# Routing one pass sooner, with halved choices and shorter steps for the last four batches

## The chip, the cores and the metric

One core of a Trainium2 chip runs the whole program. Its engines, each with a queue of its own that it works through in order, are TensorE (PE in the rows; its weight loads are PEld), VectorE (DVE), ScalarE (ACT), GpSimd (POOL) and SyncE (SP, which here only starts transfers). They wait for one another by semaphores that are written out by hand. The metric is device time in microseconds (us). All times inside the program are counted from the start of the profiled span.

## The reference, cut to what matters

`x` is 32 batches of 128 tokens by 128 features, `ctx` the same. Four blocks are added to `x` one after the other:

```python
x = x + attention_16_heads(layernorm(x), ctx)        # first attention
x = x + experts(layernorm(x))                        # 8 experts, one chosen for each token
x = x + attention_16_heads_of_64(layernorm(x), ctx)  # second attention
x = x + gated_block(layernorm(x))                    # quantised weights
```

The experts' choice (the routing) works on `i = layernorm(x)` after the first attention:

```python
num = einsum('bsd,ed->bse', i, waff)
aff = num / (norm(i) * norm(waff) + 1e-9)
tcr = one_hot(argmax(softmax(aff)))                  # the token's expert
```

Each token then goes through its expert's two matrices, if its affinity ranks high enough in its batch.

## The kernel before, in words

The program has three stages. The first is the first attention together with the routing, the second sorts the tokens by expert and runs 39 tiles of 128 tokens through the experts, the third is the second attention with the gated block.

**The first stage** is `attention_routing_block`. It runs 32 passes, one for each batch b, and every engine has its own loop over b with its own order of work. In a pass PE forms the scores of batch b, their maxima for batch b + 1 and the sums over values of batch b, and also what is left of batch b - 1: four transpositions back (`back_transposes`, L439), one more (`o_transpose`, L444) and the output product (`output`, L450). VectorE takes maxima (L720), normalises (L726, L729), adds the residual (`residual`, L735) and takes its mean and variance (`residual_stats`, L739 and L741). ScalarE copies (L533, L557, L562) and takes exponentials (L552).

**The routing of a batch r** follows its attention by some passes. It is a row of small steps on four engines:

- POOL: `route_norm(r)` adds a constant to the variance (L238), takes the power -1/2 (L240), and scales the batch to `xy` (the program's `xn2`, L244). From batch SCALED = 27 on VectorE scales (`route_scale`, L746).
- PE: `route_transpose(r)` (L336), in pass r + 4. ScalarE copies it (`route_copy`, L533). PE: `affinity(r)`, the product with `waff` (L367). VectorE copies that (`num_copy`, L628).
- For a group of batches (0 to 7, 8 to 15, 16 to 23, 24 to 27, 28 to 31): POOL computes `denominators` (L253 to L263, two powers and products), VectorE the choice in ten or so small steps (`choose`: reciprocal L634, affinity L642, and so on to the choice itself, `tcrb`, L663, and the running counts `seen`, L673), PE the place of each token (`places`, L385 to L390), VectorE the position (`locate`, L699 to L710).
- POOL: `scatter(r)` (L270) sends the batch's 128 rows to `sorted_x` in HBM, to the positions found. It sends one batch in a pass at first, two from pass 24, three from pass 29.

The tables `close_at` and `group_at` say in which pass a group's places and choice come. The choice of group 2 stands whole in VectorE's pass 27, between the residual and the copy of q (`q_spread`, L622); `route_transpose` in PE's next pass waits for that copy, since both use one PSUM bank. The choices of the last two groups come after the loops.

**The last batches.** After its loop PE works on the rest of batch 31 and on the routing of batches 29 to 31, and in between it adds up a part of the experts' constants (`expert_sums_part`, L1003, four matmuls for an expert). The count of tokens per expert (`countp`, L384) comes ahead of the places of group 4. POOL computes `denominators(4)`, and then scatters the last seven batches.

**Behind it** SP starts 18 loads for the third stage as soon as the statistics of batch 31 are known, then waits for all scatters and for the list of tiles and loads the first tiles of `sorted_x` (`e_xt`). PE has three products of weights (L1657, L1660, L1665) and then the tiles.

Of the kernel before, what the change touches and what calls it, by code (L numbers as in the profile page):

```python
# [13 lines left out]
P = 128  # L14
# [30 lines left out]
def routing_state(nc, space, ctx):  # L45
# [7 lines left out]
    def sem(name):  # L53
# [10 lines left out]
        seen=sb("seen", [P, 6, E], BF16),  # L64
        place=sb("place", [P, G, E]), posf=sb("posf", [P, B]), pos_s=sb("pos_s", [P, B], I32),
        zeros=sb("zeros", [P, 704]))
    s = {n: sem(n) for n in ("w_in", "set", "wsq", "wsum_done", "wsum", "wn", "rs2", "den", "xn2", "xnt", "xnT",
                             "num_done", "num", "choice", "place_done", "place", "z_out", "scat")}
# [3 lines left out]
def attention_routing_block(nc, ctx, space, consts, x, ctxT, w, wr, x_res, xn2, stats2, psum, dram):  # L72
# [19 lines left out]
    LATE = 28  # L92
# [49 lines left out]
    countp = xp[:, S + 16:S + 16 + E]  # L142
# [51 lines left out]
    def pool_part(g, after_setup, before_loop):  # L194
# [51 lines left out]

        def denominators(q):
# [39 lines left out]
        for b in range(B):  # L287
# [4 lines left out]
            if b >= 2:  # L292
                route_norm(b - 2)
# [19 lines left out]
    def tensor_part(pe, expert_sums_part):  # L313
# [4 lines left out]
        def x_transpose(b, s):  # L318
# [5 lines left out]
            wait(pe, rsem["num"], b - 5)  # L324
            nc.tensor.transpose(first_x(b), xn[:, s, :], ident[:]).then_inc(xt_done, 1)

        def route_transpose(r):
            pe.wait_ge(rsem["xn2"], r + 1)
            if r >= LATE:
                pe.wait_ge(mx_ready, 4 * B)  # L330
                pe.wait_ge(rsem["xnT"], r)
            else:
                pe.wait_ge(qz_ready, min(r + 6, B))
            if r == B - 5:
# [25 lines left out]
        def affinity(r):  # L360
# [4 lines left out]
            elif r + 4 in close_at:  # L365
                pe.wait_ge(rsem["place"], 4 * close_at[r + 4] + 1)
            nc.tensor.matmul(nump[r >= LATE], rt["xnT"][:, r % 2, :], rt["waffT"][:], start=True, stop=True).then_inc(rsem["num_done"], 1)  # L367

        def places(q):
# [5 lines left out]
            if q < SPREAD:  # L375
                pe.wait_ge(rsem["xnT"], z + 4)
            elif z + 5 <= B:
                pe.wait_ge(rsem["xnT"], z + 1)
# [3 lines left out]
            if q == NG - 1:  # L382
                pe.wait_ge(rsem["choice"], 10 * q + 10)
                nc.tensor.matmul(countp, rt["ones_b"][:], rt["seen"][:, q + 1, :], start=True, stop=True)  # L384
            nc.tensor.matmul(at_, rt["before_t"][:], rows[:, a:z, :].rearrange("p b e -> p (b e)"),  # L385
                             start=True, stop=False, skip_group_check=True)
            for j in range(n - 1):
# [3 lines left out]
                             start=False, stop=True, skip_group_check=True).then_inc(rsem["place_done"], 1)  # L391

# [72 lines left out]
        for b in range(B):  # L465
# [4 lines left out]
            if b >= 4:  # L470
                route_transpose(b - 4)
# [4 lines left out]
            else:  # L476
                back_transposes(b - 1, 1 - s)
            minus_max(b, 1)
            if b >= 4:
                affinity(b - 4)  # L480
# [15 lines left out]
            else:  # L496
                route_transpose(B - 4)
        affinity(B - 4)
        back_transposes(B - 1, 1)
        route_transpose(B - 3)  # L500
        places(NG - 2)
# [7 lines left out]
        route_transpose(B - 1)  # L509
        expert_sums_part(2, 3)  # L510
        affinity(B - 1)
        expert_sums_part(3, 5)
        places(NG - 1)
        expert_sums_part(5, E)

    def scalar_part(act, after_exps):
# [57 lines left out]
        for b in range(B):  # L574
# [19 lines left out]
            if b >= 3:  # L594
                route_copy(b - 3)
# [5 lines left out]
    def vector_part(dve):  # L601
# [27 lines left out]

        def choose_reciprocal(q):  # L630
            a, z = GROUPS[q]
            n, seq = z - a, rsem["choice"]
            dve.wait_ge(rsem["den"], 5 * q + 5)
# [1945 lines left out]
```

## Time and profile before

| what | us |
|---|---|
| three runs: median, lowest, highest | 808.4, 806.72, 810.31 |
| the profiled execution: its time, its span | 806.13, 804.1 |
| PE busy in the span | 758.8 (94%) |
| VectorE, ScalarE, GpSimd busy | 673.9, 439.8, 477.1 |

The span holds all of the engines' work; the time of the same execution is 2.0 us longer. The three runs differ by 3.6 us with nothing changed.

### The profile page before, as it was taken

Reading aid. Unit: us, or ns where it says so; the run is one execution under the profiler, and the core shown is the slowest. Engines: PE = TensorE matmul, PEld = TensorE weight load, DVE = VectorE, ACT = ScalarE, POOL = GpSimd, SP = SyncE. Lnnn points to the kernel's source line nnn. Section 1 sums busy time; section 2 is a strip of 40 time slices with the busy share of each in tenths; the row PEclk is TensorE's granted clock in tenths of the full one; section 3 lists DMA queues with packets and bytes.
Section 4 is the critical chain, followed back from the end, with each engine's and each line's share of the span. In section 5 each row is a group of like instructions: output and inputs, shape, how many; then the busy total and the mean of one; then the engine's idle time right before and its main releaser. Section 6 shows DMA issues by size and latency. Waiting matters only on the chain.

```text
span 804.1 us, 28859 instructions
## 1 busy us (share of the span) xinstructions
PE 758.8 (94%) x10843; PEld 639.3 (80%) x10873; DVE 673.9 (84%) x1776; ACT 439.8 (55%) x1077; POOL 477.1 (59%) x914
## 2 busy tenths in 40 slices
PE   8999999998789999899999999999999999999973
PEld 6777777766689997788888888888888888888861
DVE  5888889887767765599999999999899999999876
ACT  3666666656066663545555555655545555555442
POOL 6758578888768664244654655646546555464334
PEclk9999999999999999999999999999999999999996
DMA  8986320000422211121131221221322313213120
GB/s 239 369 344 236 146 84 15 19 15 29 145 74 63 61 47 37 39 65 45 44 87 45 61 73 46 81 52 46 87 46 60 73 45 76 57 46 78 39 44 14
DMA packets 68253, 65.81 MB, mean 82 GB/s; under 512 B 23714, under 2 KB 49042, under 8 KB 68114
## 3 DMA queue, kind: packets, MB, share of 16 engines
q1 hardware_dynamic: 53250, 39.71, 18.6%
q10 hardware_dynamic: 12816, 20.06, 6.7%
q0 software_dynamic: 2048, 4.20, 1.8%
q8 instruction: 86, 1.41, 0.7%
q14 instruction: 53, 0.43, 0.2%
HBM read 35.89 MB, written 24.37 MB: 75 GB/s over the span
## 4 chain that ended last, share of the span: by engine, by line
PE 55%; DVE 19%; DMA 12%; issue 5%; SPq 4%; POOL 3%; ACT 1%; DVEq 1%; ACTq 0%; another core or an unknown queue 0%; POOLq 0%
DMA a_r_all<-a_r_rows 6%; DMA a_r_rows<-a_rT 4%; PE psum L432 4%; PE psum L1932 4%; PE psum L1042 4%; PE psum L1816 4%; PE psum L1864 4%; SPq L1481 3%; PE psum L1832 3%; PE psum L421 3%; PE psum L1845 3%; PE psum L1898 3%; PE psum L414 3%; PE psum L1030 3%; DVE a_mxf L2273 2%
## 5 line engine op out<-in xcount | busy, mean ns | idle before, releaser
L2114 ACT ACTIVATE a_pT<-psum 128x512 f32<-128x512 f32 x128 | 69.5, 594 | 49.0 <-PE psum L1919 34.0
L720 DVE TENSOR_REDUCE l_mx<-psum 128x4 bf16<-128x512 f32 x128 | 81.9, 682 | 3.5 <-PE psum L403 1.8
L1587 POOL TENSOR_TENSOR f_hd<-f_hmc,a_wmean 128x1 f32<-128x1 f32 x32 | 6.7, 210 | 130.1 <-DVE f_hr L2373 128.8
L2273 DVE TENSOR_REDUCE a_mxf<-psum 128x8 f32<-128x1024 f32 x64 | 77.5, 1211 | 3.1 <-PE psum L1888 3.1
L1832 PEld LDWEIGHTS psum<-a_cTm,a_Wk 128*128 128x128 f32 x512 | 64.2, 191 | 19.6 <-issue 19.6
L1816 PEld LDWEIGHTS psum<-a_xT,a_Wq 128*128 128x128 f32 x512 | 64.3, 192 | 14.2 <-issue 13.4
L552 ACT ACTIVATE l_pT<-psum 128x512 f32<-128x512 f32 x128 | 70.5, 597 | 7.8 <-PE psum L421 7.5
L1581 POOL TENSOR_SCALAR f_hq<-f_ht 128x512 bf16<-128x512 f32 x31 | 60.3, 1946 | 20.0 <-ACT f_ht L2158 19.9
L1898 PE MATMUL psum<-a_qT,a_kT 64*128 64x128 f32 x1024 | 71.0, 278 | 0.0
L1832 PE MATMUL psum<-a_cTm,a_Wk 128*128 128x128 f32 x512 | 70.1, 281 | 0.0
L1864 PE MATMUL psum<-a_Wv,a_cTm 128*128 128x512 f32 x128 | 69.8, 632 | 0.1
L1816 PE MATMUL psum<-a_xT,a_Wq 128*128 128x128 f32 x512 | 69.6, 279 | 0.0
L2158 ACT ACTIVATE f_ht<-f_h,f_big_m,f_hr 128x512 f32<-128x512 f32 x32 | 26.0, 814 | 77.6 <-DVE f_hr L2373 75.5
L1932 PE MATMUL psum<-a_pT,a_v 128*32 128x128 f32 x2048 | 62.7, 274 | 0.6 <-DVE a_oT L2298 0.6
L1845 PE MATMUL psum<-a_Wo,a_oT 128*128 128x128 f32 x512 | 62.6, 275 | 0.0
L1898 PEld LDWEIGHTS psum<-a_qT,a_kT 64*128 64x128 f32 x1024 | 62.1, 188 | 0.0
L1932 PEld LDWEIGHTS psum<-a_pT,a_v 128*32 128x32 f32 x2048 | 53.9, 110 | 8.7 <-issue 5.9
L1845 PEld LDWEIGHTS psum<-a_Wo,a_oT 128*128 128x128 f32 x512 | 59.7, 192 | 0.2 <-issue 0.2
L421 PEld LDWEIGHTS psum<-negI,l_mx 128*128 128x128 bf16 x512 | 34.9, 100 | 25.0 <-DVE l_mx L720 22.7
L2145 ACT COPY a_v<-psum 128x512 f32<-128x512 f32 x64 | 37.6, 588 | 21.3 <-PE psum L1864 21.3
L1103 ACT ACTIVATE e_hT<-psum,e_w1t 128x128 f32<-128x128 f32 x156 | 44.6, 369 | 6.4 <-issue 5.7
L2298 DVE TENSOR_TENSOR a_oT<-psum,a_r_all 128x512 f32<-128x512 f32 x64 | 41.7, 678 | 7.1 <-issue 4.5
(322 smaller groups left out, 2064.1 us busy)
## 6 DMA issues: line engine op xcount, KB each, us to landing
sorted_x<-r_zeros ACTq DMA_DIRECT2D x12, 1408.0 KB, 7.0
a_r_all<-a_r_rows SPq DMA_DIRECT2D x124, 128.0 KB
e_xt<-sorted_x SPq DMA_DIRECT2D x39, 64.0 KB, 1.8
sorted_y<-e_yt ACTq DMA_DIRECT2D x39, 64.0 KB, 1.6
e_w<-in_E_W1b SPq DMA_DIRECT2D x1, 2064.0 KB
a_cin<-in_ctx SPq DMA_DIRECT2D x32, 64.0 KB, 2.7
out<-f_x SPq DMA_DIRECT2D x32, 64.0 KB, 2.3
x_res<-in_x SPq DMA_DIRECT2D x1, 512.0 KB, 5.2
```

Source lines behind the costliest of these rows:

```text
L421: last = nc.tensor.matmul(tp[k][:, j * S:(j + 1) * S], mx[:, b % 2, h:h + 1].to_broadcast([P, P]), negI[:], start=False, stop=(j == Q4 - 1 ...
L552: nc.scalar.activation(pT[:, k, :], tp[k], ACT.Exp, scale=SCALE).then_inc(exp_ready, 1)
L720: nc.vector.tensor_reduce(mx[:, s, Q4 * k:Q4 * k + Q4], maxp[k % 2].rearrange("p (h t) -> p h t", h=Q4), AX_X, ALU.max).then_inc(mx_ready, 1)
L1581: nc.gpsimd.tensor_scalar(hq[:], ht[:], -M, 127.0, ALU.add, ALU.min).then_inc(hq_ready, 1)
L1816: last = nc.tensor.matmul(bank[:, i * S:(i + 1) * S], Wq[:, 4 * half + i, :], xT[:, b % 2, :], start=True, stop=True)
L1832: last = nc.tensor.matmul(bank[:, i * S:(i + 1) * S], Wk[:, 4 * half + i, :], context_of(b), start=True, stop=True)
L1845: last = nc.tensor.matmul(pa[:, 0:D], oT[:, p, :], Wo[:, p, :], start=(p == 0), stop=(p == NP - 1))
L1864: nc.tensor.matmul(bank, context_of(b), Wv[:, 512 * half:512 * half + 512], start=True, stop=True).then_inc(v_done, 1)
L1898: last = nc.tensor.matmul(tp[e][:, i * S:(i + 1) * S], keys_of(b)[r, p, :], qT[r, b % 2, p, :], start=(half == 0 and i == 0), stop=(half = ...
L1932: last = nc.tensor.matmul(op[half][32 * j:32 * j + 32, i * S:(i + 1) * S], values_of(b)[:, 8 * half + 4 * e + i, part], pT[:, 2 * half + e ...
L2114: nc.scalar.activation(pT[:, 2 * half + e, :], tp[e], ACT.Exp, scale=SCALE).then_inc(exp_ready, 1)
L2273: nc.vector.tensor_reduce(mxf[:, 8 * half:8 * half + 8].rearrange("p (e h) -> p e h", e=2), psum[:, 0:2, :].rearrange("p e (h t) -> p e h ...
```

## The change

1. The routing of a batch stands one pass sooner: `route_transpose`, `route_copy`, `affinity` and `num_copy` of batch r in pass r + 3 instead of r + 4, with the waits that guard the shared banks moved by one. In passes 30 and 31 the transposition stands behind the four back transpositions.
2. `choose` falls into two halves. For groups 2 and 3 the first half stands in pass z + 2 and the second in pass z + 3 (z is the group's end); the choice of group 3 so comes into the loop.
3. For batches 28 to 31 VectorE forms two numbers (`spans`, variance plus a constant and variance times 128), POOL takes both powers in one instruction (`paired_roots`), and VectorE computes the last group's denominators (`last_denominators`). POOL does `denominators` for this group no more.
4. The count product stands behind the places of group 4, in another PSUM bank, and five of the eight expert sums behind it instead of three.
5. SP's 18 loads come in another order: four small ones right behind `Wv`, the wide mask and four others later, with a semaphore of their own.

```diff
+    PAIRED = GROUPS[-1][0]
...
+        def paired_roots(r):
+            i = r - PAIRED
+            g.wait_ge(rsem["spans"], i + 1)
+            nc.gpsimd.tensor_tensor(rt["roots"][:, i, :], rt["spans"][:, i, :], consts["pair"][:, 0, :], ALU.pow).then_inc(rsem["roots"], 1)
...
-            if b >= 2:
+            if b - 2 >= PAIRED:
+                paired_roots(b - 2)
+            elif b >= 2:
                 route_norm(b - 2)
...
-        route_norm(B - 2)
+        paired_roots(B - 2)
         scatter(scattered)
         scattered += 1
-        route_norm(B - 1)
-        denominators(NG - 1)
+        paired_roots(B - 1)
...
-            if q == NG - 1:
-                pe.wait_ge(rsem["choice"], 10 * q + 10)
-                nc.tensor.matmul(countp, rt["ones_b"][:], rt["seen"][:, q + 1, :], start=True, stop=True)
...
+            if q == NG - 1:
+                pe.wait_ge(rsem["choice"], 10 * q + 10)
+                nc.tensor.matmul(countp, rt["ones_b"][:], rt["seen"][:, q + 1, :], start=True, stop=True).then_inc(rsem["place_done"], 1)
...
-            if b >= 4:
-                route_transpose(b - 4)
+            if 3 <= b < SCALED + 3:
+                route_transpose(b - 3)
             if b in close_at:
                 places(close_at[b])
             if b == 0:
                 expert_sums()
             else:
                 back_transposes(b - 1, 1 - s)
+            if b >= SCALED + 3:
+                route_transpose(b - 3)
             minus_max(b, 1)
-            if b >= 4:
-                affinity(b - 4)
+            if b >= 3:
+                affinity(b - 3)
...
-            if b >= 3:
-                route_copy(b - 3)
+            if 2 <= b < B - 1:
+                route_copy(b - 2)
...
+        def last_denominators():
+            n, seq, den = B - PAIRED, rsem["den"], rt["den"][:, (NG - 1) % 2, 0:B - PAIRED, :]
+            dve.wait_ge(rsem["roots"], n)
+            nc.vector.tensor_tensor(rt["last_spread"][:], rt["roots"][:, :, 0], rt["roots"][:, :, 1], ALU.mult).then_inc(seq, 1)
+            dve.wait_ge(seq, 5 * (NG - 1) + 1)
+            nc.vector.tensor_tensor(den, rt["last_spread"][:].unsqueeze(2).broadcast_to([P, n, E]),
+                                    rt["wn"][:].unsqueeze(1).broadcast_to([P, n, E]), ALU.mult).then_inc(seq, 1)
+            dve.wait_ge(seq, 5 * (NG - 1) + 2)
+            nc.vector.tensor_scalar(den, den, 1e-9, None, ALU.add).then_inc(seq, 1)
...
+            if b >= PAIRED:
+                dve.wait_ge(x1_stats, 3 * b + 3)
+                nc.vector.scalar_tensor_tensor(out=rt["spans"][:, b - PAIRED, :], in0=consts["pair"][:, 1, :], scalar=stats2[:, b, 1:2],
+                                               in1=consts["pair"][:, 2, :], op0=ALU.mult, op1=ALU.add).then_inc(rsem["spans"], 1)
...
-            if b - 4 in group_at and SPREAD <= group_at[b - 4] < NG - 2:
-                choose(group_at[b - 4])
+            if b - 3 in group_at and SPREAD <= group_at[b - 3] < NG - 1:
+                choose_first(group_at[b - 3])
+            if b - 4 in group_at and SPREAD <= group_at[b - 4] < NG - 1:
+                choose_second(group_at[b - 4])
...
+        for i, (first, second) in enumerate(((-0.5, 0.5), (1.0, float(P)), (EPS_BLOCK, 0.0))):
+            nc.gpsimd.memset(c["pair"][:, i, 0:1], first)
+            nc.gpsimd.memset(c["pair"][:, i, 1:2], second)
```

Three places show how the order moves. The first is PE at the end of the first stage, right behind the sums over values of batch 31 (L432): L336 is `route_transpose`, L367 `affinity`, L439 the back transpositions, L444 and L450 batch 31's last two steps, L1003 the expert sums. Before, two batches' routing steps stand ahead of L444:

```order
L336 MATMUL psum<-ident,xy 128x128
L367 MATMUL psum<-r_waffT,r_xnT 128x8
L439 MATMUL psum<-ident,l_oev 128x128 x4
L336 MATMUL psum<-ident,xy 128x128
L385 MATMUL psum<-r_tcrb,r_before_t 128x32
L388 MATMUL psum<-r_tcrb,r_ones_b 128x24
L388 MATMUL psum<-r_tcrb,r_ones_b 128x16
L388 MATMUL psum<-r_tcrb,r_ones_b 128x8
L390 MATMUL psum<-r_seen,r_ones_b 128x32
L367 MATMUL psum<-r_waffT,r_xnT 128x8
L444 MATMUL psum<-ident,l_on 128x128
L450 MATMUL psum<-l_wo,l_oT 128x128
```

After (L440 is the sums over values; L390 to L395 the places, L447, L344, L375, L452 and L458 the same operations as above):

```order
L440 MATMUL psum<-l_pT,l_v 32x128 x16
L390 MATMUL psum<-r_tcrb,r_before_t 128x32
L393 MATMUL psum<-r_tcrb,r_ones_b 128x24
L393 MATMUL psum<-r_tcrb,r_ones_b 128x16
L393 MATMUL psum<-r_tcrb,r_ones_b 128x8
L395 MATMUL psum<-r_seen,r_ones_b 128x32
L447 MATMUL psum<-ident,l_oev 128x128 x4
L344 MATMUL psum<-ident,xy 128x128
L375 MATMUL psum<-r_waffT,r_xnT 128x8
L452 MATMUL psum<-ident,l_on 128x128
L458 MATMUL psum<-l_wo,l_oT 128x128
```

The transposition and the product of batch 28 have gone into pass 31, and the places of group 3 come first, since their choice now lies in the loop.

The second is the end of the same queue, from the transposition of batch 31 on. Before:

```order
L336 MATMUL psum<-ident,xy 128x128
L1003 MATMUL psum<-e_w,e_gb 128x128 x4
L367 MATMUL psum<-r_waffT,r_xnT 128x8
L1003 MATMUL psum<-e_w,e_gb 128x128 x8
L384 MATMUL psum<-r_seen,r_ones_b 128x8
L385 MATMUL psum<-r_tcrb,r_before_t 128x32
L388 MATMUL psum<-r_tcrb,r_ones_b 128x24
L388 MATMUL psum<-r_tcrb,r_ones_b 128x16
L388 MATMUL psum<-r_tcrb,r_ones_b 128x8
L390 MATMUL psum<-r_seen,r_ones_b 128x32
L1003 MATMUL psum<-e_w,e_gb 128x128 x12
```

After (L1044 is the expert sums, L399 the count):

```order
L344 MATMUL psum<-ident,xy 128x128
L375 MATMUL psum<-r_waffT,r_xnT 128x8
L1044 MATMUL psum<-e_w,e_gb 128x128 x4
L390 MATMUL psum<-r_tcrb,r_before_t 128x32
L393 MATMUL psum<-r_tcrb,r_ones_b 128x24
L393 MATMUL psum<-r_tcrb,r_ones_b 128x16
L393 MATMUL psum<-r_tcrb,r_ones_b 128x8
L395 MATMUL psum<-r_seen,r_ones_b 128x32
L399 MATMUL psum<-r_seen,r_ones_b 128x8
L1044 MATMUL psum<-e_w,e_gb 128x128 x20
```

The product of batch 31 follows its transposition at once, the count stands behind the places, and 20 matmuls instead of 12 are left behind them.

The third is VectorE from the output of batch 31 on: L735 is the residual, L739 and L741 its statistics, L628 copies a product, L746 scales. Before:

```order
L735 TENSOR_TENSOR x_res<-psum,l_xb 128x128
L739 BN_STATS l_bn<-x_res 128x6
L741 BN_AGGR stats<-l_bn 128x2
L628 COPY r_num<-psum 128x8
L746 TENSOR_SCALAR xy<-x_res,stats,r_rs 128x128
L628 COPY r_num<-psum 128x8
L634 RECIPROCAL r_tmp<-r_den 128x32
L642 TENSOR_TENSOR r_aff<-r_num,r_tmp 128x32
```

After (L761, L765, L767, L634, L781, L653 and L661 are the same operations; L770 and L639 to L644 are new):

```order
L761 TENSOR_TENSOR x_res<-psum,l_xb 128x128
L765 BN_STATS l_bn<-x_res 128x6
L767 BN_AGGR stats<-l_bn 128x2
L770 SCALAR_TENSOR_TENSOR r_spans<-pair,stats 128x2
L634 COPY r_num<-psum 128x8
L781 TENSOR_SCALAR xy<-x_res,stats,r_roots 128x128
L639 TENSOR_TENSOR r_last_spread<-r_roots 128x4
L641 TENSOR_TENSOR r_den<-r_last_spread,r_wn 128x32
L644 TENSOR_SCALAR r_den<-r_den 128x32
L653 RECIPROCAL r_tmp<-r_den 128x32
L634 COPY r_num<-psum 128x8
L661 TENSOR_TENSOR r_aff<-r_num,r_tmp 128x32
```

Four small operations are new on VectorE, and the reciprocal stands ahead of the copy of batch 31's product.

## Rows read from the trace of the kernel before

**Rows 1.** The expert stage by windows: engines' busy us (x instructions), granted clock, DMA share.

```profile
223.00:308.00 85.00, 82.05 (x705) 78.72 (x705) 57.85 (x135) 57.32 (x207) 55.92 (x83) 1.00 0.22 61
```

**Rows 2.** The chain of waits, the last batch's rows: start us, us, what.

```profile
217.12 2.79 DMA sorted_x<-xy,r_pos_s
```

**Rows 3.** The timeline of POOL: scaling of batches 24, 25 and 26.

```profile
171.21 0.81 POOL L244 TENSOR_SCALAR xy<-x_res,stats,r_rs 128x128 f32<-128x128 f32 x1
177.76 0.81 POOL L244 TENSOR_SCALAR xy<-x_res,stats,r_rs 128x128 f32<-128x128 f32 x1
184.30 0.81 POOL L244 TENSOR_SCALAR xy<-x_res,stats,r_rs 128x128 f32<-128x128 f32 x1
```

**Rows 4.** The timeline of PE: routing transpositions of passes 27, 28, 29 and 30.

```profile
170.12 0.28 PE L336 MATMUL psum<-ident,xy 128*128 128x128 f32 x1
176.97 0.30 PE L336 MATMUL psum<-ident,xy 128*128 128x128 f32 x1 [0.93 <-DVE l_qz L622]
184.09 0.28 PE L336 MATMUL psum<-ident,xy 128*128 128x128 f32 x1
189.76 0.28 PE L336 MATMUL psum<-ident,xy 128*128 128x128 f32 x1
```

**Rows 5.** The timeline of VectorE: scaling of batch 27, at the end of its pass 29.

```profile
190.34 0.33 DVE L746 TENSOR_SCALAR xy<-x_res,stats,r_rs 128x128 f32<-128x128 f32 x1
```

**Rows 6.** The timeline of ScalarE: copies in pass 30 and after the loop.

```profile
190.08 0.27 ACT L533 COPY r_xnT<-psum 128x128 f32<-128x128 f32 x1 [1.08 <-PE psum L336]
...
199.86 0.57 ACT L557 COPY l_oev<-psum 128x512 f32<-128x512 f32 x1
...
203.00 0.27 ACT L562 COPY l_oT<-psum 128x128 f32<-128x128 f32 x1 [1.06 <-PE psum L444]
```

**Rows 7.** The timeline of PE after its loop.

```profile
200.89 0.63 PE L439 MATMUL psum<-ident,l_oev 128*128 128x128 f32 x4
...
203.32 0.49 PE L450 MATMUL psum<-l_wo,l_oT 128*128 128x128 f32 x2 [0.35 <-ACT l_oT L562]
...
211.57 2.92 PE L1003 MATMUL psum<-e_w,e_gb 128*128 128x128 f32 x24
...
218.63 1.88 PE L1665 MATMUL psum<-a_Wk,a_lift_col 128*128 128x512 f32 x4
```

**Rows 8.** The timeline of VectorE after its loop.

```profile
202.29 0.29 DVE L729 TENSOR_TENSOR l_on<-psum,l_rden 128x128 f32<-128x128 f32 x1
...
204.12 0.28 DVE L735 TENSOR_TENSOR x_res<-psum,l_xb 128x128 f32<-128x128 f32 x1
...
204.77 0.18 DVE L741 BATCH_NORM_AGGREGATE stats<-l_bn 128x2 f32<-128x6 f32 x1
...
206.48 0.35 DVE L746 TENSOR_SCALAR xy<-x_res,stats,r_rs 128x128 f32<-128x128 f32 x1 [1.34 <-POOL r_rs L240]
...
209.42 0.19 DVE L642 TENSOR_TENSOR r_aff<-r_num,r_tmp 128x32 f32<-128x32 f32 x1
...
210.54 0.19 DVE L663 TENSOR_TENSOR r_tcrb<-r_score,r_smax 128x32 bf16<-128x32 f32 x1
...
211.11 0.17 DVE L673 TENSOR_TENSOR r_seen<-r_seen,r_gsum 128x8 bf16<-128x8 bf16 x1
```

**Rows 9.** The timeline of POOL after its loop.

```profile
204.43 1.08 POOL L270 DMA_INDIRECT sorted_x<-xy,r_pos_s  x1 [1.42 <-DVE r_pos_s L710]
...
205.88 0.57 POOL L240 TENSOR_TENSOR r_rs<-r_vpe,minus_half 128x1 f32<-128x1 f32 x1
...
206.95 1.05 POOL L255 TENSOR_TENSOR r_xnorm<-r_spread,half 128x4 f32<-128x4 f32 x1
```

**Rows 10.** The timeline of SP: the first of its 18 loads.

```profile
204.98 0.33 SPq L1443 DMA_DIRECT2D a_Wv<-in_A_Wv  x1
```

**Rows 11.** DMA issues from 200 to 250 us: KB each, median us to landing.

```profile
e_xt<-sorted_x SPq DMA_DIRECT2D x20, 64.0 KB, 1.8
...
a_cin<-in_ctx SPq DMA_DIRECT2D x3, 64.0 KB, 4.2
```

More of the change, by code:

```diff
@@ L64, in routing_state @@
         seen=sb("seen", [P, 6, E], BF16),
+        spans=sb("spans", [P, 4, 2]), roots=sb("roots", [P, 4, 2]), last_spread=sb("last_spread", [P, 4]),
         place=sb("place", [P, G, E]), posf=sb("posf", [P, B]), pos_s=sb("pos_s", [P, B], I32),
@@ L67, in routing_state @@
     s = {n: sem(n) for n in ("w_in", "set", "wsq", "wsum_done", "wsum", "wn", "rs2", "den", "xn2", "xnt", "xnT",
-                             "num_done", "num", "choice", "place_done", "place", "z_out", "scat")}
+                             "num_done", "num", "choice", "place_done", "place", "z_out", "scat", "spans", "roots")}
     return t, s
@@ L323, in x_transpose @@
                 pe.wait_ge(qz_ready, b)
-            wait(pe, rsem["num"], b - 5)
+            wait(pe, rsem["num"], b - 4)
             nc.tensor.transpose(first_x(b), xn[:, s, :], ident[:]).then_inc(xt_done, 1)
@@ L364, in affinity @@
                 pe.wait_ge(rsem["num"], r)
-            elif r + 4 in close_at:
-                pe.wait_ge(rsem["place"], 4 * close_at[r + 4] + 1)
+            elif r + 3 in close_at:
+                pe.wait_ge(rsem["place"], 4 * close_at[r + 3] + 1)
             nc.tensor.matmul(nump[r >= LATE], rt["xnT"][:, r % 2, :], rt["waffT"][:], start=True, stop=True).then_inc(rsem["num_done"], 1)
@@ L495, in tensor_part @@
                 max_scores(b + 1, 1)
-            else:
-                route_transpose(B - 4)
-        affinity(B - 4)
+        places(NG - 2)
         back_transposes(B - 1, 1)
         route_transpose(B - 3)
-        places(NG - 2)
         affinity(B - 3)
@@ L814, in attention_routing_block @@
     return dict(sync=sync_part, gpsimd=pool_part, tensor=tensor_part, scalar=scalar_part, vector=vector_part,
-                done=(x1_stats, 3 * B), half_done=(x1_stats, 3 * (B // 2)), exp_done=(exp_ready, 4 * B), pv_free=(oev_ready, B), actp_free=(rsem["xnT"], B), countp=countp, route=route)
+                done=(x1_stats, 3 * B), half_done=(x1_stats, 3 * (B // 2)), exp_done=(exp_ready, 4 * B), pv_free=(oev_ready, B), actp_free=(rsem["xnT"], B), countp=countp, groups=NG, route=route)
 def make_consts(nc, ctx):
@@ L823, in make_consts @@
     c = dict(ready=ready, ident=sb("ident", [P, P]), negI=sb("negI", [P, P], BF16), identb=sb("identb", [P, P], BF16),
[L824 removed]
+             mask=sb("head_rows", [P, 16]), mask4=sb("group_rows", [P, 4]), minus_half=sb("minus_half", [P, 32]), half=sb("half", [P, 32]),
+             pair=sb("pair", [P, 3, 2]))
     def pool_part(g):
@@ L1140, in floor @@
             seq.then(nc.vector.tensor_tensor(dst, dst, above, ALU.subtract))
+        dve.wait_ge(rsem["place_done"], l0["groups"] + 1)
         seq.then(nc.vector.tensor_scalar(ne[:], l0["countp"], float(P - 1), 1.0 / P, ALU.add, ALU.mult))
@@ L1455, in sync_weights @@
         sp.dma_start(cin2[:], w["ctx"][2]).then_inc(cin_ld[0], 16)
+        sp.dma_start(mrow8[:], w["mask"].partition_broadcast(P)).then_inc(late_in, 16)
+        for t, n in ((s1, "ln1_s"), (b1, "ln1_b")):
+            sp.dma_start(t[:], w[n].rearrange("(d a) -> d a", a=1)).then_inc(late_in, 16)
+        sp.dma_start(so_row[:], w["lno_s"].partition_broadcast(P)).then_inc(late_in, 16)
+        sp.dma_start(bo_row[:], w["lno_b"].partition_broadcast(P)).then_inc(late_in, 16)
         sp.dma_start(wf[:, 0, :], wff["gateT"]).then_inc(f_in, 16)
```

74 lines of the change are left out of this document (44 added, 30 removed).

## The prediction

> **What bounds the kernel now.** I began at the end of the first stage, because all edits lie there, and asked who waits for it. The window of the expert stage shows TensorE (PE) busy 82.05 of 85 us [rows 1]. PE works there without a gap that could take up a shift, so the end of the program moves one for one with the first tile of that stage. The chain of waits behind that tile ends in the last batch's rows, whose transfer starts at 217.12 and takes 2.79 us [rows 2]. Behind them SP loads the tile. What counts is therefore how early the places of batches 28 to 31 are known, and whether GpSimd's (POOL's) queue and the transfers then follow.
>
> Next I read the timelines of the passes, since a step that is moved one pass sooner must have its input one pass sooner. The reader is to compare two groups. POOL finishes scaling batch 24 at 171.21 + 0.81 = 172.02, batch 25 at 178.57 and batch 26 at 185.11 [rows 3]. PE transposed one batch in each pass, at 170.12 (pass 27), 176.97 (28), 184.09 (29) and 189.76 (30) [rows 4]. Before, pass 28 took batch 24, which had been ready for 5 us. Afterwards pass 27 takes batch 24, pass 28 batch 25, pass 29 batch 26. POOL is late in just these passes, because from pass 24 on it sends two batches in each and in pass 25 has the denominators of group 2 as well.
>
> **Passes 27 to 29.** In pass 27 PE waits from 170.12 to 172.07, 1.95 us. Pass 28's transposition came 6.85 later, of which 0.93 was a wait for VectorE's copy of q [rows 4]. That wait goes, because only half of the choice now stands ahead of the copy; 172.07 + 5.92 = 177.99. But batch 25 is ready only at 178.6, and this bound wins: 1.6 later than 176.97. The gain of the halved choice is swallowed here. In pass 29 PE would come at 184.09 + 1.6 = 185.7, and batch 26 is ready at 185.11: no further wait. Loss 1.6 (bounds: 1.0, if only pass 27's wait less the 0.93 counts; 2.0).
>
> **Passes 30 and 31.** Batch 27 is scaled by VectorE at the end of its pass 29, at 190.34 + 0.33 = 190.67 [rows 5]. VectorE is 1.6 late by then and has a new small operation ahead (`spans`; I take 0.17, as the smallest operation on 8 columns [rows 8]), so about 192.45. PE now puts the back transpositions first: they start at 189.76 + 1.6 = 191.35 and take about 0.4 until the next can start, which makes 191.75. It waits 0.7. The copy on ScalarE starts 0.32 after the transposition (189.76, 190.08) and takes 0.27 [rows 4, 6]; between transposition and product PE has one group of matmuls, some 0.35, and waits 0.25 more. That is 1.0 in pass 30. Pass 31 repeats it with batch 28; I take 0.8, since VectorE is close behind there anyway. Bounds 0 (if VectorE's pass 29 shrinks) and 1.2 each. All passes together: the loop ends 1.6 + 1.0 + 0.8 = 3.4 later. Since the product and transposition of one more batch stand in the first passes, all is about 0.2 later still.
>
> **After the loop.** Here most edits pay. I follow one path, from the last ScalarE copy of the loop to the places.
>
> - Copy ready (199.86 + 0.57 = 200.43) to residual (204.12): 3.69 [rows 6, 8]. In between VectorE had group 3's choice and position, and PE a wait for batch 28. Both are gone. What is left: back transpositions 0.63, normalising 0.29 and a reciprocal like it, a transposition 0.3, a copy 0.27, the product 0.49 [rows 4, 6 to 8], five handovers of 0.05 and 0.15 behind batch 29's product: 2.65. Gain 1.05.
> - Residual to scaling (206.48): 2.36 [rows 8]. The statistics ended at 204.95, but POOL was sending batch 24 until 205.51 [rows 8, 9]. That row now goes out earlier. POOL's two operations become VectorE's 0.2 and one power of two columns. The trace has no such power: one column takes 0.57, four take 1.05 [rows 9]. I take 0.73, by the line between them, and so no difference to the 0.97 from 205.51 to 206.48. Gain 0.5 (0.2 to 0.65).
> - Scaling to the affinities (209.42): 2.94 [rows 8], held by POOL's denominators. Now it is scaling 0.35, transposition 0.3, copy 0.27, product 0.3, copy 0.17 and five handovers: 1.6. VectorE's four new steps (about 1.0 with the reciprocal) lie beside it. Gain 1.35.
> - The places waited for `seen` (211.11 + 0.17); the choice itself was there at 210.73 [rows 8]. Gain 0.55.
>
> Together 3.45. The places thus end where they ended before: 3.4 lost, 3.45 gained.
>
> **Behind the places.** POOL's last seven sends stood behind its denominators, whose power alone ended at 208.0 [rows 9]; three small steps later, from about 209.4 to the start of the last at 217.12 [rows 2], they took 1.3 each, and the fourth started at 213.3. The position (four small VectorE steps of 0.2 behind the places) was there at about 212.6. Now the denominators are gone and the last four sends follow the position by 0.3: 0.4 sooner. PE has five expert sums left instead of three, 2.92 / 3 each [rows 7], 2 us more, and is free at 218.63 + 1.88 + 2 = 222.5 at the latest [rows 7]. The last rows land near 217.12 + 2.79 = 219.9, and SP's issue (about 1) and the load (1.8 [rows 11]) bring the first tile to 222.7. The two are close; I give this edit nothing, and up to 0.5 in the range.
>
> The 18 loads of SP start when batch 31's statistics are done: at 204.98 before [rows 10], and now 3.4 - 1.05 = 2.3 later. So the loads reach further over the last sends. A 64 KB load in that stretch took 4.2 us, a tile's load behind it 1.8 [rows 11]: being among the loads can cost up to 2.4. I take 0.8, a third, since the last transfer already began among them. The Trainium skill (DMA: Bandwidth & Descriptors, section on queues, rings and completion order) says that each DMA engine takes turns, a packet at a time, between the queues that have work. By that alone the 2.79 would at most double and the sum would come out 2 us higher; no row here shows the turns.
>
> Edits at nothing: six memsets of one column at POOL's start (hidden, as PE's first projection waits for its weights' transfer; six of POOL's smallest operations without that cover), and the new semaphore of the loads, whose first reader comes behind the fourth expert tile.
>
> **Sum.** 3.4 + 0.2 - 3.45 - 0.4 + 0.8 = +0.55 on the profiled execution's 806.13: 806.7. The median of the runs shown is 808.4; the mean over these three and the profiled one is 807.9. From that I forecast 808.4. What a measurement can tell from no change here is about 0.5%, 4 us.
>
> **Rivals.**
>
> - *The passes do not wait.* Then the loop ends 0.9 sooner than before, and the tail's gain stands until POOL's own queue of sends bounds it. I put that at 3.4 in all: 804.5. For it: the halved choice removes a real 0.93. Against it: rows 3 against rows 4. Chance 0.18.
> - *Every pass from 27 on waits as pass 27 does* (slower). Each wait of PE makes VectorE's statistics late, these POOL's next scaling, and that PE again. It decides if batch 26 is scaled later than 185.7. Three more waits of 1.95 in place of the 1.8 forecast are 4.0 more: 812.4. Against it: POOL scales batches 24 to 26 at an even 6.5 us [rows 3], set by its own queue and not by VectorE. Chance 0.10.
> - *The loads hold back the last rows.* By the skill's turns above, or by the 2.4 of the rows: 1.6 to 2 more than taken, 810.2. Chance 0.12.
> - The forecast's own case: 0.60; 806 to 810.8 with the bounds above and the spread of the runs.
>
> Range 804.3 to 811.8. Faster by over 0.5% (below 804.4) needs a bit under half of the first rival and a tail of my own case, 0.11; slower (above 812.4) half of the second and little of the third, 0.07; the same 0.82.
>
> **What would show it.** In pass 27 PE's transposition waits near 2 us for POOL, and no wait for the copy of q is left in pass 28. In passes 30 and 31 it waits for VectorE's scaling. The loop's last sums over values end 3.4 later than before, the choice of group 4 comes near 210.7 as before, and the last transfer of rows takes over 3 us. I am wrong if that choice comes before 209 or after 212, or if PE's products hold the first tile.

## The result, and the profile after

The changed kernel takes 812.74 us (median of 17 runs, 809.92 to 817.45), the kernel before in the same comparison 808.82 (805.82 to 812.64). The ratio on record is 1.0064, 95% interval 1.0047 to 1.0081 (the two medians alone give 1.0048): slower, and above the range of the prediction. In a second comparison it was 1.0043 (1.0015 to 1.007). The profiled execution takes 815.37, its span is 813.6 (before 804.1). The profile of after is thus a long run of its kernel and the profile of before (806.13) a short one, so that the two profiles lie 9.2 us apart and the medians 3.9.

To compare the two traces I count from the sums over values of batch 26, the last ones ahead of the passes in which the prediction saw new waits: 167.62 before, 166.10 after. So 1.52 is to be added to a time of after, which makes it a time on the clock of before. The sums over values of batches 26 and 31 before (L432), and of batches 26, 27 and 31 after (L440):

```profile
167.62 1.08 PE L432 MATMUL psum<-l_pT,l_v 128*32 128x128 f32 x32
...
198.29 1.08 PE L432 MATMUL psum<-l_pT,l_v 128*32 128x128 f32 x32 [0.38 <-DVE x_res L735]
```
```profile
166.10 1.08 PE L440 MATMUL psum<-l_pT,l_v 128*32 128x128 f32 x32
...
175.28 1.08 PE L440 MATMUL psum<-l_pT,l_v 128*32 128x128 f32 x32
...
202.21 1.08 PE L440 MATMUL psum<-l_pT,l_v 128*32 128x128 f32 x32 [0.38 <-DVE x_res L761]
```

From batch 26 to batch 31 it is 30.67 us before and 36.11 after, so the loop ends 5.4 later.

First PE in passes 27, 28 and 30 (L344 is the routing transposition, L447 the back transpositions, L440 the sums over values):

```profile
170.55 0.35 PE L344 MATMUL psum<-ident,xy 128*128 128x128 f32 x1 [1.79 <-POOL xy L246]
170.71 1.04 PE L447 MATMUL psum<-ident,l_oev 128*128 128x128 f32 x4
...
177.77 0.28 PE L344 MATMUL psum<-ident,xy 128*128 128x128 f32 x1
...
191.75 0.33 PE L344 MATMUL psum<-ident,xy 128*128 128x128 f32 x1 [0.67 <-DVE xy L781]
...
194.73 1.93 PE L440 MATMUL psum<-l_pT,l_v 128*32 128x128 f32 x32 [0.47 <-DVE x_res L761]
```

The waits of passes 27 and 30 are those forecast: 170.55 + 1.52 = 172.07 for batch 24, and 0.67 for batch 27. Pass 28 has no wait, neither the 0.93 for the copy of q of [rows 4] nor the 0.6 for batch 25 that the prediction put in its place. New is what stands behind the waits: the four back transpositions take 1.04 (0.63 in [rows 7]), the values of batch 30 1.93, where batch 27's took 1.08 in the same trace. The windows tell why (columns as in [rows 1]: busy us of PE, weight loads, VectorE, ScalarE, POOL, then the granted clock):

```profile
172.00:174.00 2.00, 2.00 (x20) 1.72 (x19) 1.76 (x7) 1.08 (x3) 1.52 (x3) 0.50 0.00 0
196.00:198.00 2.00, 2.00 (x32) 1.05 (x20) 0.77 (x2) 0.59 (x1) 1.68 (x3) 0.50 0.12 41
228.00:230.00 2.00, 1.65 (x9) 1.24 (x7) 0.94 (x5) 0.39 (x2) 0.00 (x0) 0.50 0.12 34
...
227.00:312.00 85.00, 82.12 (x687) 78.79 (x688) 56.56 (x132) 57.28 (x207) 55.71 (x79) 0.97 0.21 60
```

Up to the first tiles three stretches stand at 0.50, the lower level (1.2 GHz). The expert stage shows PE as busy as in [rows 1], but in the same 85 us the trace has 687 matmuls instead of 705, and its first tile comes 5.2 us later (226.48 + 1.52 against 222.78).

Behind the loop, VectorE (L761 residual, L781 scaling, L661 affinity, L682 the choice):

```profile
206.90 0.29 DVE L761 TENSOR_TENSOR x_res<-psum,l_xb 128x128 f32<-128x128 f32 x1 [0.84 <-PE psum L458]
...
208.83 0.34 DVE L781 TENSOR_SCALAR xy<-x_res,stats,r_roots 128x128 f32<-128x128 f32 x1 [0.60 <-POOL r_roots L252]
...
210.61 0.19 DVE L661 TENSOR_TENSOR r_aff<-r_num,r_tmp 128x32 f32<-128x32 f32 x1
...
211.73 0.19 DVE L682 TENSOR_TENSOR r_tcrb<-r_score,r_smax 128x32 bf16<-128x32 f32 x1
```

Then the loads of SP, first and last, and the chain of waits (its answers to [rows 2]):

```profile
207.76 0.33 SPq L1486 DMA_DIRECT2D a_Wv<-in_A_Wv  x1
...
215.72 0.43 SPq L1505 DMA_DIRECT2D f_wf<-in_F_downT  x1
```
```profile
217.28 6.08 DMA sorted_x<-xy,r_pos_s
...
224.42 1.93 DMA e_xt<-sorted_x
```

On the clock of before the last send starts at 218.80 instead of 217.12, 1.7 later, and its rows land 6.08 us behind it instead of 2.79. The load of the tile takes 1.93 instead of 1.69. That makes up the 5.2 of the first tile. The last of SP's loads, before and then after (KB, us from issue to landing, as in [rows 11]):

```profile
f_wf<-in_F_downT SPq DMA_DIRECT2D x1, 256.0 KB, 6.1
```
```profile
f_wf<-in_F_downT SPq DMA_DIRECT2D x1, 256.0 KB, 7.6
```

After, it is issued at 215.72, so it lands within 0.1 us of the last rows (217.28 + 6.08 = 223.36). PE at the first tile, before and then after (L1712 is the last product of weights, L1022 and L1063 the tile's transposition, L1030 and L1071 its products):

```profile
222.78 0.30 PE L1022 MATMUL psum<-ident,e_xt 128*128 128x128 f32 x1 [2.27 <-DMA e_xt<-sorted_x]
223.43 1.16 PE L1030 MATMUL psum<-e_xtT,e_w1t 128*128 128x128 f32 x8 [0.36 <-ACT e_xtT L1092]
```
```profile
220.61 1.88 PE L1712 MATMUL psum<-a_Wk,a_lift_col 128*128 128x512 f32 x4
226.48 0.45 PE L1063 MATMUL psum<-ident,e_xt 128*128 128x128 f32 x1 [3.99 <-DMA e_xt<-sorted_x]
227.28 2.08 PE L1071 MATMUL psum<-e_xtT,e_w1t 128*128 128x128 f32 x8 [0.36 <-ACT e_xtT L1133]
```

PE idles for 3.99 us instead of 2.27 and then works at half clock: the first tile's eight products take 2.08 instead of 1.16, and from the first tile's products to the third's it is 5.7 us instead of 3.7.

### The profile page after: what moved, and what is told of

The parts are those of the page before. It is cut to its first block, busy times and chain, and to the rows that moved or that the text cites. A ratio compares the mean times of both kernels' runs of the same rounds, so it can differ in the third digit from the quotient of the medians.

```text
span 813.6 us, 28894 instructions
## 1 busy us (share of the span) xinstructions
PE 770.6 (95%) x10873; PEld 643.2 (79%) x10873; DVE 678.1 (83%) x1783; ACT 439.8 (54%) x1077; POOL 473.2 (58%) x911
## 4 chain that ended last, share of the span: by engine, by line
PE 33%; DVE 31%; DMA 19%; issue 7%; SPq 6%; POOL 3%; ACT 1%; DVEq 1%; POOLq 0%; ACTq 0%
DMA a_r_all<-a_r_rows 10%; DMA a_r_rows<-a_rT 7%; SPq L1528 6%; DVE a_mxf L2323 4%; PE psum L1083 4%; PE psum L440 4%; DVE a_rT L2339 3%; PE psum L429 3%; PE psum L1071 3%; PE psum L422 3%; DVE a_oT L2348 3%; DVE f_h L2412 3%; DVE f_hm L2418 2%; DVE f_xt L2397 2%; PE psum L411 2%
## 5 line engine op out<-in xcount | busy, mean ns | idle before, releaser
L746 DVE TENSOR_REDUCE l_mx<-psum 128x4 bf16<-128x512 f32 x128 | 81.8, 681 | 3.5 <-PE psum L411 1.9
```

The lines of the kernel that those rows point to most:

```text
L746: nc.vector.tensor_reduce(mx[:, s, Q4 * k:Q4 * k + Q4], maxp[k % 2].rearrange("p (h t) -> p h t", h=Q4), AX_X, ALU.max).then_inc(mx_ready, 1)
```

## The experiments

Each kernel ran 12 times (late_loads 6) beside the kernel before on the same chip; ratios are to that one, in brackets the 95% interval. These shared a chip each: passes_only to filled; spaced, tail_spaced, filled_spaced and old_order; loads_only to old_again; fill_first to tail_spaced2; the last two.

**The change in parts.** passes_only has edits 1 and 2, tail_only edits 3 and 4; both have the old order of loads, with the loads' own semaphore of edit 5. The edits are shown in part.

```diff
# passes_only, against the changed kernel
-            if b - 2 >= PAIRED:
-                paired_roots(b - 2)
-            elif b >= 2:
+            if b >= 2:
...
# tail_only, against the changed kernel
-            if 3 <= b < SCALED + 3:
-                route_transpose(b - 3)
+            if b >= 4:
+                route_transpose(b - 4)
...
```

> The kernel before with edits 1 and 2 alone: the routing a pass sooner and the choice in halves; the last group's powers, denominators, count and the loads as before. The theory that the passes cost (waits for POOL and VectorE in passes 27 and 30, and behind each a stretch of PE at half the granted clock): the loop's last sums over values come 5 to 5.5 us later than before and the tail gives back about 1 (group 3's choice has left it); the loads shift with the sends, so the last transfer stays near 2.8 us: 812 to 814. The rival that the loss lies in the transfers behind the loop alone: the passes' own loss is small, 808 to 810.

> The kernel before with edits 3 and 4 alone: paired powers, VectorE's denominators for the last group, the count behind the places; routing in pass r + 4, whole choices and the loads' order as before. If the passes cost the time: no wait for POOL in pass 27, a granted clock of 1.00 up to the end of the stage, and the tail's gain is free, 0.5 + 1.35 + 0.55 for the places and 0.4 for the sends, of which what POOL's queue of sends lets through: 2 to 3 us, 806 to 807. If the last rows are held by the loads whatever the passes do: the last transfer takes 4 us or more and the time stays at 808 to 809.5.

passes_only: 808.91, 1.0017 (0.999 to 1.0044). tail_only: 806.79, 1.0003 (0.9974 to 1.0033). Neither alone costs what the whole does, and the tail alone does not bring its 2 to 3 us. The chains, passes_only first, then tail_only:

```profile
219.87 2.22 DMA sorted_x<-xy,r_pos_s
```
```profile
216.37 4.79 DMA sorted_x<-xy,r_pos_s
```

In passes_only the last load starts at 216.38, 3.5 us ahead of the last send; in tail_only at 214.09, 2.3 ahead. So sends that come sooner behind the same loads wait longer. Each run takes one sign from either of its expectations: passes_only has the short transfer and the time of the rival, tail_only the long transfer and the lower time. In tail_only, whose passes are those of before, the clock also fell behind pass 28's wait for the copy of q (0.95), where it had not in the profile of before. tail_only, then before:

```profile
178.00:180.00 2.00, 2.00 (x20) 1.74 (x15) 1.47 (x4) 1.16 (x5) 1.75 (x2) 0.50 0.00 0
```
```profile
178.00:180.00 2.00, 1.62 (x29) 1.42 (x26) 1.83 (x11) 0.67 (x2) 1.81 (x4) 1.00 0.00 0
```

**The loads behind the first tiles.**

```diff
             load(i)
+        late_loads()
         sp.wait_ge(from_dve, CDS)
```

> The changed kernel, with the 13 loads from nk_row on started behind the loads of the first six tiles. If the loads hold back the last rows: the last transfer falls from 6.1 to about 2.8 us or less, the first tile's product starts 3.3 us sooner, and with a shorter wait the granted clock stays near 1.00 behind it, which is up to 2 more: 407 is no wait any more, the time 807.5 to 809.5. If the last rows are late for another reason (POOL's queue, the sends' own time): 812 to 813 as the changed kernel, and the last transfer still over 5 us.

(The words on 407 in it are a slip.) 816.69, 1.0116 (1.0077 to 1.0155): slower. But its two halves point apart. The transfer is as short as the first theory said, and the first tile's transposition starts at 221.73, 4.75 us sooner than in the changed kernel. PE then stands at the seventh tile, behind the loads that I put in its way:

```profile
216.56 2.23 DMA sorted_x<-xy,r_pos_s
```
```profile
237.69 0.47 PE L1064 MATMUL psum<-ident,e_xt 128*128 128x128 f32 x1 [4.28 <-DMA e_xt<-sorted_x]
```

**PE kept busy in its waits.**

```diff
+    FILL = {24: 6, 27: 3, 28: 2}
...
+            for _ in range(FILL.get(r, 0)):
+                nc.tensor.matmul(xnp[r >= LATE], ident[:], ident[:], start=True, stop=True)
+            pe.wait_ge(rsem["xn2"], r + 1)
...
+        for _ in range(12):
+            nc.tensor.matmul(xtp[:, 0:P], ident[:], ident[:], start=True, stop=True)
         x_transpose(0)
```

> The changed kernel with products of the identity that nobody reads, in the places where PE waits: six ahead of the transposition of batch 24 (pass 27), three ahead of batch 27's, two ahead of batch 28's, twelve ahead of the first tile. They go to PSUM that is written anew right after. The waits stay as long as they are. If the clock costs time by itself: the granted clock stays at 1.00 in 170 to 174, 194 to 198 and 225 to 232, the values of batch 30 take 1.08 instead of 1.93, and the time falls by 3 to 5 us, to 808 to 810. If the low clock only coincides with waits that would end at the same time anyway: 812 to 813; if the products get in the way, slower.

809.28, 1.0028 (1.0006 to 1.0049), 0.15 to 0.36% below the changed kernel's two ratios, with more work on PE; the intervals overlap. The clock holds through the loop and at the first tiles, and batch 30's values take 1.08 at the very time at which they took 1.93:

```profile
194.73 1.08 PE L443 MATMUL psum<-l_pT,l_v 128*32 128x128 f32 x32 [0.47 <-DVE x_res L764]
```
```profile
172.00:174.00 2.00, 2.00 (x28) 1.85 (x27) 1.93 (x7) 1.81 (x6) 1.82 (x2) 1.00 0.00 0
```

**The large loads one by one behind the seventh to twelfth tile.** spaced is the changed kernel, tail_spaced edits 3 and 4, filled_spaced has the unread products in the passes too.

```diff
             if i + XT < NT:
                 load(i + XT)
+            spaced_load(i)
```

> The changed kernel, with the six largest of the late loads (the wide mask, the three wf, so_row and bo_row) started one by one behind the seventh to twelfth tile's load; the small ones and cin stay where they are. In the run before, all late loads behind the sixth tile's load, the last transfer fell to 2.23 us but the seventh tile stood behind them for 5 us. If the loads hold the last rows: last transfer 2 to 3 us, first tile's product 3.5 to 5 us sooner than in the changed kernel, no wait of PE at the seventh tile, and 807.5 to 809.5. If the time is lost elsewhere, 811 or more with the transfer short.

> Edits 3 and 4 alone, with the loads spaced as in spaced. With edits 3 and 4 alone and the loads as before, the last send started 0.75 us sooner than in the kernel before but its transfer took 4.79 instead of 2.79. If that collision hides the tail's gain: the transfer takes 2 to 3 us, the first tile comes 1 to 1.5 us sooner than before (counted from the values of batch 26), and the time is 804.5 to 806.5. If not: 806.5 to 808.5.

> The changed kernel with the loads spaced and with the unread products of filled in passes 27, 30 and 31 (none ahead of the first tile). Filled alone took 2.9 off the changed kernel's ratio and left the last transfer at 5.4 us. If clock and loads are two separate losses they add: 805 to 807.5. If each only uncovers the other: 808 to 809.5.

spaced: 807.67, 0.999 (0.9966 to 1.0013), so 0.5 to 0.7% below the changed kernel. The tile is there before PE is, 3.9 sooner than in the changed kernel and without a wait:

```profile
222.56 0.30 PE L1064 MATMUL psum<-ident,e_xt 128*128 128x128 f32 x1
```

tail_spaced: 805.9, 0.9956 (0.9932 to 0.9981), faster than both kernels. filled_spaced: 808.65, 0.9993 (0.9968 to 1.0017): no more than spaced. The two do not add: the first tile has no wait for its rows there either, PE's own queue of expert sums comes last, at half clock in 214 to 216.

**Edit 5 alone undone, alone done, and with the tail.**

```diff
# old_order, old_again, against the changed kernel, behind Wv
+        for t, n in ((s1, "ln1_s"), (b1, "ln1_b")):
...
         for t, n in ((sc_, "lnc_s"), (bc, "lnc_b")):
...
-        sp.dma_start(nv_col[:], w["nv2"]).then_inc(w_in, 16)
...
+        sp.dma_start(nv_col[:], w["nv2"]).then_inc(w_in, 16)
         for b in range(2):
```

loads_only is the kernel before with edit 5 (its count product writes the PSUM bank of edit 4), tail_loads has edits 3, 4 and 5.

> The changed kernel with edit 5 alone undone: the 18 loads in the order of before, started when they are in the changed kernel. If only their lateness counts (last load started about 1 us ahead of the last send): the last transfer still takes over 5 us, 812 to 813. If their new order counts, because it puts the wide mask next to the last rows: 4 us or less, 809.5 to 811.

> The kernel before with edit 5 alone (the new order of the loads, with their own semaphore). Passes alone gave a ratio of 1.0017, tail alone 1.0003, both without edit 5 1.001, all three 1.0064. If edit 5 costs by itself, whatever stands around it: 1.004 to 1.006, 812 to 813.5. If it costs only where the loads lie close to the last sends: here the last load starts about 4 us ahead of the last send, the last transfer takes 2.8 to 3.5 us, and the time is 808 to 809.5.

> Edits 3, 4 and 5 without the passes. With the old order the last transfer took 4.79 us in this arrangement and the ratio was 1.0003. If the new order puts more bytes next to the last rows (wide mask and wf, 1.3 MB, are all among the last nine loads): transfer over 5.5 us, ratio 1.003 to 1.006. If the order counts for nothing: 0.998 to 1.002.

> The changed kernel once more, beside the others on one chip. If the ratio of 1.0064 is the kernel's: 1.005 to 1.008. If it was that chip's: 1.001 to 1.004, and then nothing is left to explain by edit 5.

> The changed kernel with the old order of loads once more, beside the changed kernel on one chip. If edit 5 costs: 0.3 to 0.6% below it. If the chips differ more than the kernels: within 0.2% of it.

old_order: 809.56, 1.001 (0.9988 to 1.0033); old_again: 810.98, 1.0008 (0.9984 to 1.0033), beside after_again: 813.5, 1.0043 (1.0015 to 1.007). loads_only: 809.51, 0.9978 (0.9956 to 0.9999); tail_loads: 809.61, 0.9989 (0.9959 to 1.0019). So edit 5 costs 0.35% with all the others (on one chip; 0.54% between the first ratios) and nothing that can be seen without the passes; what it does with the passes alone was not tried. The last transfer takes 5.72 in old_order, 3.77 in old_again, 4.16 in loads_only and 6.28 in tail_loads; so tail_loads, too, has the long transfer, and is not slower than before. Part of the cost is seen at PE, old_again:

```profile
218.68 2.05 PE L1704 MATMUL psum<-a_Wo,a_nv_col 128*128 128x128 f32 x16 [0.39 <-DMA a_nv_col<-in_A_nv]
...
225.06 0.30 PE L1063 MATMUL psum<-ident,e_xt 128*128 128x128 f32 x1 [0.90 <-DMA e_xt<-sorted_x]
225.72 1.16 PE L1071 MATMUL psum<-e_xtT,e_w1t 128*128 128x128 f32 x8 [0.35 <-ACT e_xtT L1133]
```

In the old order the three products wait for nv_col, a late load (0.39 here, 1.14 in old_order), start 5.1 and 5.9 us behind the count (L399), and end less than 1 us before the tile. In the new one they start 4.6 us behind the count in both profiles of the changed kernel, PE idles for 3.9 to 4.0, and the first tiles run at half clock. The rows also land later in the new order, 7.6 us behind the start of the last load against 6.3 and 7.3. That this idle time is the whole cost is not shown: loads_only idles for 3.71 and runs its first tiles at half clock too, and its ratio is 0.9978.

**That idle time alone closed, and the square of passes and tail without the loads.** fill_first is the changed kernel with the twelve unread products ahead of the first tile only; tail_spaced2 and all_spaced2 have

```diff
-        expert_sums_part(2, 3)
+        expert_sums_part(2, 4)
         places(NG - 1)
-        expert_sums_part(3, E)
+        expert_sums_part(4, E)
```

> The changed kernel with twelve unread products of the identity (3.4 us) ahead of the first tile and nothing else changed. The changed kernel's ratio was 1.0064 and 1.0043; PE stood idle for 3.9 us there in both profiles and the first tiles ran at half the granted clock, 5.4 to 5.7 us from the first tile's products to the third's instead of 3.7. If that low clock is edit 5's cost: the steps are 3.7 again and the ratio falls to 1.002 to 1.004, the tile itself no sooner. If the cost lies elsewhere: 1.005 or more.

> The kernel before with the loads spaced as in spaced (and edit 5's order for the rest). tail_spaced had 0.9956. If the tail's edits gain once no load is in the way: this one lies 0.2 to 0.4% above it, 0.998 to 1.0. If spacing alone brings it and the tail's edits nothing: 0.995 to 0.997.

> Edits 1 and 2 alone with the loads spaced. If the passes cost 3 to 4 us of the loop's end whatever follows, less 1 in the tail: 0.3% above before_spaced, 1.001 to 1.003, above spaced (0.999) by what the tail's edits gain. If the passes cost nothing by themselves: as before_spaced.

> tail_spaced (0.9956) with two expert sums instead of one ahead of the last places and four behind them. In tail_spaced PE came to the first tile without a wait for it. If PE's own queue bounds the first tile there: 0.5 to 1 us sooner, 0.994 to 0.9955. If the places come later by what is put ahead of them: 0.9956 to 0.997.

> The changed kernel with the loads spaced and two expert sums ahead of the last places: tail_spaced2 with the passes. If the passes cost by themselves what the loop's end showed (3.9 us later over the profiles, less 0.8 in the tail): 0.996 to 0.998, 0.3 to 0.5% above tail_spaced2. If they cost only through the loads and the sums: within 0.1% of it.

> tail_spaced2 once more. If its 0.993 is the kernel's: 0.991 to 0.996 again, and still below the kernel before and the changed one.

fill_first: 811.68, 1.0029 (1.0003 to 1.0055), 0.14 to 0.35% below the changed kernel, with intervals that overlap; filled, which closes the same gap, has 1.0028. In fill_first the granted clock is 1.00 at the first tiles, from 226 on, and from the first tile to the third it is 3.7 us. before_spaced: 807.03, 0.996 (0.9932 to 0.9987). passes_spaced: 808.22, 0.9992 (0.9965 to 1.0019). tail_spaced2: 803.53, 0.993 (0.9904 to 0.9957), again 805.14, 0.9957 (0.9933 to 0.998). all_spaced2: 807.31, 0.9981 (0.9959 to 1.0003).

The passes cost 0.3% (passes_spaced over before_spaced) and 0.24% (all_spaced2 over tail_spaced2 on its chip): 2 to 2.6 us, each less than its intervals can tell by itself. The tail's edits give 0.02% (spaced, passes_spaced, on different chips), and with four sums behind the places 0 to 0.3% (tail_spaced2 twice, before_spaced); their size stays open. PE's queue, tail_spaced first, then tail_spaced2, shows that the sums held the first tile in one profile (there partly at half clock) and the rows in the other:

```profile
211.69 6.07 PE L1046 MATMUL psum<-e_w,e_gb 128*128 128x128 f32 x39
...
222.81 0.27 PE L1065 MATMUL psum<-ident,e_xt 128*128 128x128 f32 x1
```
```profile
211.83 3.40 PE L1046 MATMUL psum<-e_w,e_gb 128*128 128x128 f32 x29
...
221.32 0.30 PE L1065 MATMUL psum<-ident,e_xt 128*128 128x128 f32 x1 [0.86 <-DMA e_xt<-sorted_x]
```

tail_spaced2 has the lowest ratio of this study, but its second measurement lies level with tail_spaced and before_spaced.

## Why the prediction was wrong

**Right: the waits of the passes.** Pass 27 waits 1.79 (1.95 forecast), pass 29 not at all, pass 30 0.67 (0.7). The 0.6 forecast for batch 25 in pass 28 is missing in this profile, because the half clock behind pass 27's wait had already made PE that late. It stands as 0.57 to 0.66 in the four profiles in which the clock held there (all_spaced2, fill_first, filled, filled_spaced). No run of the passes shows the rival in which every pass waits.

**Mis-sized against its own profile: the loop's end, +3.4 and 0.2.** From batch 26's values to batch 31's it is 36.11 in the changed kernel's profile and 30.67 before: 5.4. Most of the missing part is the clock, which the prediction priced nowhere: 9.18 instead of 5.76 + 1.95 from batch 26's values to batch 27's, and 0.85 more for batch 30's, of which pass 28's missing wait gives some back. Where the unread products hold the clock (filled, filled_spaced), the distance is 34.78 and 34.74, which is 4.1 above before; so the waits are worth 4.1 (3.6 forecast), and the clock costs 1.3 more. But the profile of before was a lucky one. In eight profiles with its passes the distance is 30.67 to 33.81, mean 32.40, and its own is the lowest, since in the seven others the clock fell behind pass 28's wait. In nine profiles with the new passes and no unread products it is 34.96 to 37.20, mean 36.05. The difference of the means, 3.65, is the forecast's 3.6, and that is luck: the forecast left the clock out on both sides. The change takes away one stretch of half clock (pass 28) and makes another, behind pass 27 in eight of the nine and behind pass 30 in three. The runs without a trace say the same of the profile of before: in 157 of them on record, median 809.3, the mean granted clock is 0.990 or more, as in that profile, in only seven.

**Right: the steps of the tail.** Copy ready to residual 2.61 (2.65), residual to scaling 1.93 (1.86), the pair of powers 0.72 (0.73), scaling to affinities 1.78 (1.6). From the loop's end to the last send the tail gained 3.8 (5.4 later has become 1.7), as forecast (3.45 + 0.4). The choice came at 211.73 + 0.19 + 1.52 = 213.4 on the clock of before. By the prediction's own terms it stood at 211.4 and not "near 210.7 as before", since 0.55 of the 3.45 lies behind the choice; most of the other 2.0 is the loop, which in this profile ended 1.8 later than forecast.

**Wrong: "the 18 loads ... I take 0.8, a third".** This step failed: against the profile of before the transfer cost 3.3 more (6.08 against 2.79) and not 0.8. The last rows do not land a little later than their send plus 2.79; they land with the loads. From the start of the last load to the landing it is 7.64 (changed kernel), 7.61 (again), 7.83 (tail_loads), 7.86 (filled) and 8.26 (loads_only) in the new order, wherever the last send stood, 1.5 to 4.1 us behind that start. In the old order it is 6.3 to 7.3 (old_again 6.34, before 6.91, tail_only 7.07, old_order 7.27); only passes_only, whose send is 3.5 behind, lands 2.22 after its send (5.71 behind the last load's start), as long as a transfer without loads beside it takes. The loads start with batch 31's statistics, which the passes make later, by 4.3 (207.76 + 1.52 against 204.98) and not by the 2.3 forecast, and from there loads and landing take some 15.6 us in the new order (207.76 to 223.36). The tail's gains in choice and sends lie inside these 15.6 us, so they were added to the sum but did not bring the landing forward; only the gain ahead of the statistics (residual) did. The third rival named the right mechanism, with a price that stopped at 2.4, from the 4.2 of one load [rows 11], and a chance of 0.12. The Trainium skill (DMA: Bandwidth & Descriptors, section on queues, rings and completion order) says that a DMA engine takes turns between queues; the prediction estimated from it that the 2.79 would at most double, to 5.6. The runs agree that loads on SP's queue slow POOL's transfer, but not with that bound: it takes 2.2 with no loads beside it and 6.1 to 6.3 among them. The turns themselves no run shows.

In terms of the forecast's sum, the last send was to come 0.25 sooner (3.4 + 0.2 - 3.45 - 0.4) and came 1.7 later, by the loop's end; the loads were to add 0.8 and added 3.3. So the first tile was to come 0.55 later and came 5.2 later.

**Wrong: "Edits at nothing".** The new order of loads was priced by its readers, and it cost 0.35 to 0.54% (old_again, old_order). A part of that lies with PE: the products get their small inputs sooner, which no one needed, the rows land later, and PE has 3.9 us of idle time ahead of the first tile. Closing that gap alone takes 0.14 to 0.35% off. The rest of the price, and why the same gap costs nothing in loads_only, stays open. The products' early end was even in the prediction, as a bound (free at 222.5 at the latest).

**The sum as the runs give it.** spaced against the two ratios of the changed kernel: the loads and the idle time ahead of the first tile cost 0.5 to 0.7%, 4 to 6 us, of which 1 to 3 seem to be the clock there (fill_first). What is left, spaced at 0.999, is the passes' loss against what before_spaced shows that a kernel without that collision gains (0.4%). Why before gains that much from it, although its one profile shows a transfer of 2.79, stays open: there is no second profile of it. Open is also the rest of the program, from the first tile to the end of the span, which differs by some 8 us between profiles with nearly the same code there (late_loads left out); between the profiles of before and after it is 5.8, of which the half clock at the first tiles is 2.0.

## What to carry to other kernels

A step that comes sooner gains only if nothing else that ends at the same place starts later: here the gain ran in parallel with a burst of loads, and the burst had its start behind the loss. Ask of every new wait of PE what the clock does behind it, and price both levels. One profile is one execution: the profile before lacked a stretch of half clock that all seven others with the same passes had.

## What the runs showed of the hardware

The granted clock falls behind waits that look harmless, and not every time. In pass 28 of the old passes a wait of 0.93 and one of 0.56 left it at 1.00 in one profile, and it stood at 0.50 for some us behind nearly the same waits (0.94 to 0.97 and 0.56) in seven. In pass 27 of the new passes it fell behind a wait of 1.78 to 1.81 in eight profiles, and not behind 1.78 (all_spaced2) and 1.88 (fill_first) in two. Ahead of the first tile it fell behind waits of 2.0, 2.6, 3.7, 3.9 and 4.0 us, once behind 1.4 (passes_spaced), and not behind 0.9, 1.6, 1.8, nor behind 2.3 (before). A wait's length alone does not tell it.

A transfer of 64 KB of scattered rows took 2.2 us by itself and up to 6.3 among loads that had been issued before it: a queue of its own did not keep it from waiting for theirs. In the changed kernel it landed 7.64 us behind the start of the last of these loads, which itself took 7.6.
